# Moving three items of TensorE's slot schedule: normed rows' transposes, one key projection, and the second attention's value-weight product

## Time and profile before

| what | value |
|---|---|
| median of 3 runs | 1106.21 us (1103.28 to 1108.82) |
| span of the profiled execution | 1134.4 us |
| PE busy in it | 1039.8 us (92%) |
| DVE busy | 813.1 us (72%) |
| ACT busy | 716.6 us (63%) |
| POOL busy | 521.5 us (46%) |
| one steady period (one batch, 16 slots) | 52.81 us |

### The profile page before, as it was taken

One profiled execution on the slowest core, in us unless ns is written; L12 is line 12 of the kernel. 1 busy time (PEld: TensorE's weight loads), 2 busy tenths in 40 slices (PEclk: granted clock), 3 DMA queues, 4 the chain that ended last, 5 costly groups with the idle time before them and its releaser, 6 DMA issues. The chain is left out here.

```text
span 1134.4 us, 22413 instructions
## 1 busy us (share of the span) xinstructions
PE 1039.8 (92%) x7055; PEld 957.5 (84%) x7055; DVE 813.1 (72%) x2017; ACT 716.6 (63%) x1853; POOL 521.5 (46%) x747
## 2 busy tenths in 40 slices
PE   4899999999999999999999999999998778859995
PEld 4899898989889988889898988898897767858993
DVE  4656786868777787878686878677876865846665
ACT  4645766676766767676767676676766545635661
POOL 5413245445454635454545445463534225544441
PEclk9999999999999999999999999999998889989999
DMA  6332122222323232222222222212213522344469
GB/s 175 99 110 59 43 57 65 56 63 59 78 56 81 53 79 65 69 61 61 64 54 70 60 53 58 64 50 62 54 46 93 180 62 89 116 111 156 135 191 315
DMA packets 77569, 98.47 MB, mean 87 GB/s; under 512 B 14459, under 2 KB 69373, under 8 KB 77200
## 3 DMA queue, kind: packets, MB, share of 16 engines
q1 hardware_dynamic: 68064, 79.04, 26.3%
q0 software_dynamic: 8848, 16.96, 4.3%
q10 hardware_dynamic: 544, 1.05, 0.3%
HBM read 44.08 MB, written 23.03 MB: 59 GB/s over the span
## 5 line engine op out<-in xcount | busy, mean ns | idle before, releaser
L935 POOL TENSOR_TENSOR prob<-prob,rinv 112x750 f32<-112x750 f32 x128 | 184.1, 1438 | 250.3 <-DVE rinv L1609 239.8
L1027 ACT ACTIVATE prob<-ps_s,negmax 112x375 f32<-112x375 f32 x256 | 143.9, 570 | 61.5 <-DVE negmax L1603 52.4
L1616 DVE TENSOR_TENSOR pT_lo<-ps_pt,pT_hi 125x672 fp32r<-125x672 f32 x128 | 108.5, 847 | 63.1 <-ACT pT_hi L1164 57.7
L1707 PE MATMUL ps_kv<-ctxT_hi,wkv 128*128 128x376 f32 x512 | 138.5, 351 | 2.1 <-DVE v_lo L1276 1.4
L1603 DVE TENSOR_REDUCE negmax<-ps_s 112x2 f32<-112x750 f32 x128 | 119.0, 930 | 1.6 <-PE ps_s L1955 1.5
L1707 PE MATMUL ps_kv<-wkv,ctxT_hi 128*125 128x512 f32 x384 | 110.7, 410 | 2.4 <-DVE k_low L1272 2.4
L1017 ACT ACTIVATE v_hi<-ps_kv 125x512 fp32r<-125x512 f32 x96 | 57.3, 597 | 80.9 <-PE ps_kv L1707 75.8
L894 POOL DMA_INDIRECT places<-ysb,place_i x72 | 70.9, 984 | 81.1 <-issue 43.0
L1965 PE MATMUL ps_pt<-ident,prob 112*125 112x112 f32 x768 | 104.4, 272 | 2.3 <-POOL prob L935 2.3
L1164 ACT ACTIVATE pT_hi<-ps_pt 125x672 fp32r<-125x672 f32 x128 | 93.6, 731 | 5.7 <-PE ps_pt L1965 1.1
L1965 PEld LDWEIGHTS ps_pt<-ident,prob 112*125 112x125 f32 x768 | 94.8, 190 | 2.6 <-POOL prob L935 2.5
(11 more groups left out here) (312 smaller groups left out, 2752.8 us busy)
## 6 DMA issues: line engine op xcount, KB each, us to landing
kx<-k_low SPq DMA_DIRECT2D x256, 94.0 KB
xg<-rows_by_expert SPq DMA_DIRECT2D x72, 128.0 KB
qx_hi<-qx_hi SPq DMA_DIRECT2D x64, 112.0 KB, 2.2
zb<-places SPq DMA_DIRECT2D x16, 448.0 KB, 15.7
ctx_in<-in_ctx SPq DMA_DIRECT2D x16, 375.0 KB
stage_w<-in_L_ffn_mlp_w SPq DMA_DIRECT2D x16, 256.0 KB, 5.3
arena<-in_L_ffn_mlp_w SPq DMA_DIRECT2D x16, 256.0 KB, 5.8
stage_w<-in_L_xattn_w_kv SPq DMA_DIRECT2D x4, 512.0 KB, 11.9
```

What stands on the lines that cost most here:

```text
L935: e_prob.done(eng.tensor_tensor(prob[0:TQ, p % 2, :, :], prob[0:TQ, p % 2, :, :], rinv[:, 2 * p:2 * p + 2].unsqueeze(2).broadcast_to([TQ, ...
L1027: e_exp.done(eng.activation(prob[0:TQ, p % 2, half, :], S[0:TQ, half, 0:SK], ACT.Exp, bias=negmax[:, h:h + 1], accum_out=rowsum[:, h:h + 1]))
L1616: e_pt_lo.done(eng.tensor_tensor(pT_lo[:, :, :, :].rearrange("p h k t -> p h (k t)"), PT[0:KEYT, :, 0:NKEY * TQ], pT_hi[:, :, :, :].bitcas ...
L1707: last = eng.matmul(out_, lhs(i, k), rhs(j, k), start=(n == 1), stop=(n == KT * len(PASSES)))
```

## The change

In `KV_AT`, the `x` group goes from slot -5 to slot -8 (modulo 16: from 11 to 8) and the key group of pair 1 from -1 to -2 (from 15 to 14). `AT_XN` goes from -8 to -9 (from slot 8 to slot 7). Tail piece 8 goes from `T_EARLY` to `T_LATE` at the same slots, so that it is issued behind slot 14's projection group and no longer ahead of it. ScalarE's wait for gamma moves with the `x` group. After it the groups stand: 7: k5, e; 8: x; 9: v4, k6; 10: k7, v5; 11: c0; 12: c1; 13: q0, k0; 14: k1; 15: v0.

```diff
-        KV_AT = (("v", 1, 0), ("x", 0, -5), ("k", 2, 1), ("q", 0, -3), ("r", 0, 36), ("k", 7, 10),
+        KV_AT = (("v", 1, 0), ("x", 0, -8), ("k", 2, 1), ("q", 0, -3), ("r", 0, 36), ("k", 7, 10),
                  ("v", 3, 6), ("q", 1, 3), ("v", 4, 9), ("c", 0, -5), ("c", 1, -4), ("k", 5, 7),
                  ("k", 0, -3), ("v", 2, 2), ("e", 0, 39), ("k", 4, 5), ("v", 5, 10), ("k", 6, 9),
-                 ("k", 3, 3), ("k", 1, -1), ("v", 0, -1))
+                 ("k", 3, 3), ("k", 1, -2), ("v", 0, -1))
...
-        AT_LN, AT_XN, AT_XB0 = -10, -8, 3
-
-        T_EARLY = ((0, 20, 20), (1, 22, 21), (6, 29, 27), (8, 30, 28), (9, 32, 30), (10, 34, 30))
-        T_LATE = ((2, 22, 21), (3, 24, 23), (4, 25, 24), (5, 26, 25), (7, 29, 27))
+        AT_LN, AT_XN, AT_XB0 = -10, -9, 3
+
+        T_EARLY = ((0, 20, 20), (1, 22, 21), (6, 29, 27), (9, 32, 30), (10, 34, 30))
+        T_LATE = ((2, 22, 21), (3, 24, 23), (4, 25, 24), (5, 26, 25), (7, 29, 27), (8, 30, 28))
...
             for g in range(FIRST, LAST):
-                if g == -5:
+                if g == -8:
                     eng.wait_ge(ld_ln, 32)
```

## The result

The changed kernel takes **1194.6 us** (median of 4 runs, 1191.05 to 1195.04), the one before, run beside it, 1104.74 us (1101.27 to 1108.82): a ratio of 1.0781, 95% interval 1.0745 to 1.0816 (the two medians by themselves stand at 1.0813). It is slower by 89.9 us, where the forecast had 35.4 and a range of 1112 to 1151.

A forecast was written before the change was run, and what follows sets the result against it. PE's queue was taken to bound the kernel. Per batch 2.85 - 1.46 + 0.6 + 0.2 + 0.3 = 2.49 us; 13 such batches plus two with 1.0 less gave 35.4, and 1106.2 + 35.4 = 1141.6 us, range 1112 to 1151.

The forecast's parts named there:

- The likeliest case: Whole kernel: the new waits outweigh the removed ones, 35.4 us slower, 1141.6 us; chance 0.62.
- wait of `x` in slot 8: PE, slot 8: `x` waits for k5's `k_low`, delayed by `xn` and POOL's hold; 2.85 us in 13 batches.
- the same in the other two: Periods 0 and 1, no `e` in front: `x` waits for `xn`, O(2) for `pT_lo`; 1.85 us.
- removed waits (c1, piece 8, v1): PE, slots 12, 14 and 0: three waits vanish, 0.81, 0.48 and 0.17, together 1.46 us a batch.
- O(4): PE, slots 11 and 12: O(4) reached earlier, then waits for `pT_lo` of pair 4; 0.6 us a batch.
- k1 for q0's bank: PE, slot 14: k1 waits until `qx_lo` has released q0's bank; 0.2 us a batch, 0.3 at most.
- tail piece 9: PE, slots 14 and 15: piece 9 waits for the later normed rows; 0.3 us a batch, between 0 and 0.5.
- What happens is shown twice: DVE, slot 7: one-column operations overlapping POOL's end with it, 0.68 and 2.10 us instead of 0.21; so would `refine`'s second step.
- A: DVE, slot 7: POOL does not hold `refine`; wait 1.6 for 2.85, 17 us in all, 1123 us; chance 0.18.
- B: Whole batch: new waits cancel the old 1.46 us; 1106 us, O(2) at about 431.0; chance 0.09.
- C: DVE, slot 7: `xn` is hidden, `k_low` still ends at 429.84; 8 us faster, 1098 us; chance 0.11.
- D: Slot 14: one wait takes another's place; counted in the forecast, no chance of its own.

The follow-up runs named there:

- the fill: The changed kernel with 16 unused matmuls of 376 columns ahead of the `x` group in slot 8, from the third period on; 1156.3 us, ratio 1.0432.
- `xn` alone: The kernel before with only `xn` moved to slot 7, `x` staying in slot 11; 1171.1 us, ratio 1.0566.
- one-input kernel: The changed kernel with both `refine` steps ahead of `xn` as `tensor_scalar` with one SBUF tensor instead of two; 1157.7 us, ratio 1.0477.
- `e` in slot 6: The changed kernel with group `e` one slot earlier, so `x` no longer takes k5's bank; 1149.0 us, ratio 1.0395.
- `x` half: The kernel before with only `x` moved to slot 8 and `xn` to slot 7, k1 and tail piece 8 left; 1178.0 us, ratio 1.0623.
- 8 matmuls: The changed kernel with 8 unused matmuls of 376 columns ahead of `x` in slot 8; 1163.1 us, ratio 1.0509.

## Why the prediction was wrong

The sign and the waits in slots 7 and 8 held; what such a wait does to the clock was missing, and with it the size. The likeliest case said 1141.6 us, and 1194.6 came. Step by step, in us a batch:

| step of the forecast | forecast | measured | by |
|---|---|---|---|
| wait of `x` in slot 8, 13 batches | +2.85 | +3.22 | the wait row (41.8 / 13) |
| the same in the other two | +1.85 | +2.7 and +0.7 at `x` | the wait row; the trace at 47 us |
| removed waits (c1, piece 8, v1) | -1.46 | -0.3 | the kernel before, profiled again |
| O(4) | +0.6 | +0.43 | its timeline row |
| k1 for q0's bank | +0.2 | 0 | no such row |
| tail piece 9 | +0.3 | +0.33 | its wait row |
| half clock behind the wait | not in the sum | +3.0 | the fill, 38.7 / 13 |

The measured column sums to 6.7 for a batch of the first kind, and the 13 periods grew by 6.4 each (83.1 / 13). The 0.3 between them I can't place. Over the whole run the forecast's loss was 35.4 us and the measured one 89.9; the clock, the removed waits and the 0.37 at `x`, less what O(4) and k1 were put too high, account for the 54.5 between them to within some 2 us.

**The step that failed** is the first: "Wait added: 2.85 us", costed at its own length. The forecast took PE's clock from the earlier trace rows as a constant of the kernel, though it made PE stand still for longer in one piece than any wait in the earlier trace rows. The clock was the largest missing term, 38.7 us of 83.1, and none of the forecast's ranges held it. That this is the clock and not a wait in disguise is shown twice, by work that made no wait end earlier: the useless matmuls gave back 38.3 us in the changed kernel and 30.4 in the one with `xn` alone.

**The second is a term mis-sized**, "What it takes away": 1.46 us, with 0.3 to be had. The rows were read rightly, but they came from an execution whose span lay 28 us above the median. That was written down, and carried over as if the surplus were evenly spread. It wasn't: 18.3 us of the 23.7 between the two profiled spans lay in the 13 periods, at least in part in just the waits that the change was to remove. This accounts for 1.16 x 15 = 17 us of the miss.

The steps behind "What happens is shown twice" held. Line 1292 takes 1.38 us in the `ln_h` form, 1.4 forecast, and ends with POOL's scaling. (One of the two examples was weaker than it was taken for: the operation of 2.10 us, line 1382 in the earlier trace rows, had started 0.62 us ahead of POOL's and is the only long one of 16.) What was missed there is `xn`, put at its 0.41 us of a quiet place: POOL's next operation, `xb`, follows at once and holds it to 0.78. That is the 0.37 between 2.85 and 3.22. The Trainium skill (SBUF — State Buffer, section "Who interferes with whom") would have given this too, since by it a `tensor_scalar` can also take the shared ports in a fast mode that needs both; the forecast used only its two-input half. These traces agree with it: in the one-input kernel the single-column steps pass, and the 256-column one is held. No run changes that mode by itself.

Of the rivals, A (no hold by POOL) is refuted by line 1292. B needed O(2) at about 431.0 and C a `k_low` of k5 that ends at 429.84, as in the earlier trace rows; here `k_low` holds `x` for 3.2 us after PE's last scores. Of D, the exchange of one wait for another in slot 14, only tail piece 9's new wait came. The period was forecast at some 55.3; it is 58.03, and 55.05 when the clock is kept up. That 55.05 lies so near 55.3 is luck: the forecast added 2.49 us to 52.81, where the runs show 3.41 on top of 51.64.

## What to carry to other kernels

A wait on the engine that bounds the kernel can be priced at its length only while it is short. Here one standstill of TensorE of 2.5 to 3.2 us in each period also slowed what followed, so look at the clock line first, and where it falls, cost such a wait at up to twice its length. Before moving small VectorE operations a slot earlier, look at what GpSimd does in that slot, and what stands behind them in the queue. And if the profiled execution lies well above the median, don't count on small waits read from it.

## What the runs showed of the hardware

- **The clock has a price with steps.** A standstill of 3.2 us in each period of 58 was followed by 6.8 us at 0.50 in every one of them. With 2.5 us (`xn` alone, one-input steps) the low stretch was 0, 3.4 or 6.8 us; with 1.8 it came in 4 of 13 periods; with 1.5 (`e` in slot 6) in one; with 0.8 in none. That more than the length of one wait counts is shown by the `x` half: the same 3.2 us wait, but a low stretch of only 3.4 us in eight of 13 periods. What decides it in a given period stays open. The Trainium skill (TensorE: Matmul & The Clock Gate, section "HAM oscillation — how this bites in real kernels") reckons such a stretch to cost half its length; by that an estimate for 6.8 us is 3.4. The fill showed 3.0, and PE still stood for the first 0.46 us of the stretch. With 8 matmuls a stretch of 3.4 us cost 1.6 (56.6 less 55.05).
- **POOL's hold passes from one instruction to the next.** `xn` (112 x 256, fp32, one SBUF tensor) took 0.41 us alone, 0.78 beside `xb` and 1.21 beside `prob`. Beside either it ended about 0.15 us behind POOL's operation. One-column operations with one input weren't held: 0.25 and 0.21 us beside `prob`, where one with two inputs took 1.38.
- **More matmuls made the kernel faster.** 16 useless ones a period, 208 in the 13 periods, took 38.3 us off the time. As a mend it isn't worth having here, since the wait that they cover costs more than the change can bring.
